# TensorE's projections on other slots, and one state transposed per slot

## What is computed

```python
x = x + _L0_attn_ref(_layernorm(x, axis=-1), ...)
x = x + _L0_ffn_ref(_layernorm(x, axis=-1), ...)
...
xz = x @ in_proj_w.T
xc, z = jnp.split(xz, 2, axis=-1)
...   # u: full convolution over 4 tokens and 512 channels of xc
dt = jnp.clip(jax.nn.sigmoid(u @ dt_w.T + dt_b), 0.0001, 1.0)
A = -jnp.exp(A_log)
Bm = u @ B_w.T
Cm = u @ C_w.T
def step(state, inp):
    dA = jnp.exp(jnp.clip(dtt[:, :, None] * A, -5.0, 5.0))
    dB = dtt[:, :, None] * bt[:, None, :] * ut[:, :, None]
    state = dA * state + dB + 1e-06
    y = jnp.sum(state * ct[:, None, :], axis=-1) + D * ut
...
y = y * jax.nn.silu(z)
return y @ out_w.T
...   # ffn: top 2 of 8 experts by softmax, silu(gate) * up, down; plus a gated shared expert
```

## Time and profile before

| | |
|---|---|
| median of 3 runs | 2993.37 us (2986.91 to 2995.44) |
| profiled execution | 2990.34 us |
| its span, first to last instruction | 2988.5 us |
| mean granted clock of TensorE | 0.915 of full |
| PE busy | 2630.8 us, 88% |
| PEld busy (weight loads) | 2312.5 us, 77% |
| DVE busy | 2249.8 us, 75% |
| ACT busy | 2033.5 us, 68% |
| POOL busy | 2235.5 us, 75% |

### The profile page before, as it was taken

One profiled execution on the slowest core, in us unless ns is written; L12 is line 12 of the kernel. 1 busy time (PEld: TensorE's weight loads), 2 busy tenths in 40 slices (PEclk: granted clock), 3 DMA queues, 4 the chain that ended last, 5 costly groups with the idle time before them and its releaser, 6 DMA issues. The chain is left out here.

```text
span 2988.5 us, 49244 instructions
## 1 busy us (share of the span) xinstructions
PE 2630.8 (88%) x15616; PEld 2312.5 (77%) x15616; DVE 2249.8 (75%) x4890; ACT 2033.5 (68%) x4675; POOL 2235.5 (75%) x1354
## 2 busy tenths in 40 slices
PE   7888898889888888988988888898886599999998
PEld 4777787778777777877877877887875488888887
DVE  2999889988998999899889989998999233333332
ACT  3987888888878888788878878888876133333332
POOL 2999888988888889889889988898887033333333
PEclk9999989998999888899899899888997699999999
DMA  4222222222222222222222222222221278888886
GB/s 168 82 75 76 75 82 76 75 75 90 88 80 79 75 79 89 76 76 85 79 76 75 76 82 75 75 89 87 78 74 41 75 199 201 202 201 202 198 204 152
DMA packets 138185, 309.67 MB, mean 104 GB/s; under 512 B 15041, under 2 KB 79681, under 8 KB 137793
## 3 DMA queue, kind: packets, MB, share of 16 engines
q1 hardware_dynamic: 110848, 270.03, 28.9%
q0 software_dynamic: 27072, 36.46, 6.2%
HBM read 258.42 MB, written 48.01 MB: 103 GB/s over the span
## 5 line engine op out<-in xcount | busy, mean ns | idle before, releaser
L1032 POOL TENSOR_TENSOR room<-dtu,b_all 128x1024 f32<-128x1024 f32 x512 | 1202.3, 2371 | 32.4 <-DVE dtu L1420 14.1
L810 ACT ACTIVATE bank<-room,eps_col 128x512 f32<-128x512 f32 x1024 | 695.2, 685 | 294.6 <-DVE carry L1257 200.3
L794 ACT ACTIVATE room<-room,neg_a 128x256 f32<-128x256 f32 x2048 | 868.8, 499 | 0.8 <-DVE room L1209 0.8
L600 PE MATMUL bank<-ident,room 128*128 128x128 f32 x4096 | 550.9, 291 | 242.7 <-DVE room L1252 220.1
L600 PEld LDWEIGHTS bank<-ident,room 128*128 128x128 f32 x4096 | 495.3, 150 | 295.9 <-DVE room L1252 238.8
L1021 POOL TENSOR_TENSOR room<-room,c_all 128x1024 f32<-128x1024 f32 x224 | 530.9, 2370 | 159.3 <-DVE bank L1243 59.8
L1243 DVE TENSOR_TENSOR_SCAN bank<-room,carry,bank 128x256 f32<-128x256 f32 x864 | 580.3, 735 | 54.5 <-ACT bank L810 53.7
L1157 POOL DMA_INDIRECT out<-room,ids x144 | 223.8, 1554 | 410.1 <-DMA out<-room,ids 192.9
L1322 DVE SCALAR_TENSOR_TENSOR hid<-hid,bank 128x256 f32<-128x256 f32 (+1 forms) x312 | 131.0, 420 | 453.5 <-ACT hid L905 421.2
L1243 DVE TENSOR_TENSOR_SCAN room<-room,carry,bank 128x256 f32<-128x256 f32 x672 | 445.7, 726 | 0.7 <-DVE hot L1293 0.5
L552 PE MATMUL bank<-xnT,w_conv 128*128 128x256 f32 x3072 | 404.2, 288 | 7.0 <-ACT xnT L833 5.5
(11 more groups left out here) (150 smaller groups left out, 3151.0 us busy)
## 6 DMA issues: line engine op xcount, KB each, us to landing
b_all<-b_scratch SPq DMA_DIRECT2D x128, 512.0 KB, 3.9
c_all<-b_scratch SPq DMA_DIRECT2D x128, 512.0 KB, 5.1
room<-in_wgu SPq DMA_DIRECT2D x72, 704.0 KB, 5.8
room<-in_wd SPq DMA_DIRECT2D x72, 384.0 KB
room<-x_by_expert SPq DMA_DIRECT2D x72, 260.0 KB
x_in<-in_x SPq DMA_DIRECT2D x32, 256.0 KB, 5.9
x<-in_x SPq DMA_DIRECT2D x32, 256.0 KB, 2.7
out<-x SPq DMA_DIRECT2D x32, 256.0 KB, 4.2
```

The costliest lines, as they stand in the source:

```text
L600: last = mm(tr_bank[k][:, b * P:(b + 1) * P], v[n % VRING][:, b, k * P:(k + 1) * P], ident[:, :], is_transpose=True, start=False, stop=(n ...
L794: last = af(da[n % RING][:, b, :], dt[c.par][:, b, :], ACT.Exp, scale=neg_a[:, b, n:n + 1])
L810: af(v_slot(c, n, h)[:, :], v[n % VRING][:, 2 * h:2 * h + 2, :].rearrange("p b t -> p (b t)"), ACT.Identity, bias=eps_col[:, 0:1]).then_in ...
L1032: nc.gpsimd.tensor_tensor(out=v[n % VRING][:, :, :], in0=dtu[:, :, :], in1=row, op=ALU.mult) \
```

## The change

- `CONV_SLOT` becomes [0, 4, 5] and holds the last three groups. The first group of a chunk is done at slot 15 of the round before, when the chunk is still in the norm role; for chunks 0 and 1 it is called in `start`.
- b and c go from slot 5 to 7, dt from 6 and 7 to 7 and 8, z from 9 and 10 to 10 and 11, gate and up from 11, 12, 13 to 12, 13, 14, on TensorE.
- ScalarE takes the results at 1 and 6 (uT), 7 (b and c), 8 and 9 (dt), 11 and 12 (z). The gates are at 13, 14, 15 on ScalarE and VectorE. VectorE's `proj_dt` goes to 9 and 10, `proj_gate` to 12, `low_normed` from 15 to 14.
- TensorE transposes state n at slot n + 2, one in each slot. Before, it did two in every even slot. States 14 and 15 stay at slot 0 of the next round.

```diff
-GU_SLOT, GATE_SLOT = [11, 12, 13], [12, 13, 14]
+GU_SLOT, GATE_SLOT = [12, 13, 14], [13, 14, 15]
-CONV_SLOT, Z_SLOT = [0, 1, 3, 4], [9, 10]
+CONV_SLOT, Z_SLOT = [0, 4, 5], [10, 11]
+DT_SLOT, BC_SLOT = [7, 8], 7
...
                 if slot in CONV_SLOT:
-                    n = CONV_SLOT.index(slot)
+                    n = CONV_SLOT.index(slot) + 1
                     proj_conv(c, n // 2, n % 2)
-                if slot == 5:
+                if slot == BC_SLOT:
                     proj_bc(c)
-                if slot in (6, 7):
-                    proj_dt(c, slot - 6)
+                if slot in DT_SLOT:
+                    proj_dt(c, DT_SLOT.index(slot))
...
+                    proj_conv(Chunk(0, 0), 0, 0)
                     for slot in range(NS):
                         project(Chunk(0, 0), slot)
                     proj_norm(Chunk(0, 1))
+                    proj_conv(Chunk(0, 1), 0, 0)
...
-                        if slot > 0 and slot % 2 == 0 and scan:
+                        if slot > 1 and scan:
                             state_transpose(scan, slot - 2)
-                            state_transpose(scan, slot - 1)
...
+                        if norm and slot == 15:
+                            proj_conv(norm, 0, 0)
...
-                if slot in (2, 5):
-                    h = slot // 3
+                if slot in (1, 6):
+                    h = slot // 6
...
-                if slot in (7, 8):
-                    h = slot - 7
+                if slot in (8, 9):
+                    h = slot - 8
...
-                if slot == 6:
+                if slot == 7:
...
-                if slot in (10, 11):
-                    k = slot - 10
+                if slot in (11, 12):
+                    k = slot - 11
...
-                        if slot == 8:
+                        if slot == 9:
                             decays(Chunk(0, 0), 0)
...
-                        if proj and slot in (8, 9):
-                            proj_dt(proj, slot - 8)
-                        if proj and slot == 11:
+                        if proj and slot in (9, 10):
+                            proj_dt(proj, slot - 9)
+                        if proj and slot == 12:
                             proj_gate(proj, 0)
                             proj_gate(proj, 1)
-                        if norm and slot == 15:
+                        if norm and slot == 14:
                             low_normed(norm)
```

## The result

The changed kernel takes **3018.5 us** (median of four runs, 3016.4 to 3021.1), against 2993.2 of the kernel before, run beside it on the same chip (2986.9 to 2995.4). The ratio is 1.0088 with a 95% interval of 1.0071 to 1.0106, so it is slower by 25 us, a little under 1%. That is outside my range and on the other side of my forecast. The profiled execution took 3021.1 us (span 3019.4), 30.8 more than the one before.

What follows compares the result with a forecast made beforehand. No engine owns the loop; VectorE's short repeated waits hang on a chain through the others. Terms 0.98 + 0.8 + 0.5 - 0.6 - 1.4 = 0.3 us mid-sequence, mean 0.5, 15 us over 30 chunks: 2978 us, range 2950 to 3012.

Steps and rivals of the forecast that it cites:

- A: Rival, chance 0.18: bc waits for later uT, TensorE's clock falls, dt and z are late; 1.7 us per chunk, 3029.
- Against it: one wait of 3.29 us left the clock at 1.00: Argument against the clock-fall rival: in the trace before, a 3.29 us wait did not lower TensorE's clock.
- two idle stretches of 3.6 us with little between them: Argument for the clock-fall rival: these TensorE idle stretches bring the clock down at 1044, full again from 1054.
- One transpose per slot: TensorE's state transposes cost the same and GpSimd's buffers keep over 2 us at most slots: zero on both sides.
- The conv group to slot 15: Conv falls into TensorE's wait for state 15, so VectorE's output-product wait goes: gain 0.98 us per chunk.
- Conv and two transposes just fit: On TensorE, 3.2 + 0.95 + 0.95 us fit between second and third gate; down starts at about 0.15.
- uT later: uT's second half behind both ScalarE copies shortens VectorE's state 7 waits from 1.93 to 1.16: gain 0.8 us.
- b/c and dt later: VectorE no longer waits for dt's tanh, 0.6; state 9's second copy stays late: gain 0.5 us.
- z later: VectorE's wait for the second z's tanh after state 12 grows to 0.95 us: loss 0.6 us per chunk.
- The low part a slot earlier: VectorE waits 1.3 us, 1.4 with overlap, for ScalarE's copy behind state 14's products: loss 1.4 us per chunk.
- a low clock over dt's matmuls: Sign named as showing the forecast wrong, on TensorE: it would mean the clock-fall rival; no size given.
- z's wait far over 1 us: Sign named as showing the forecast wrong, on VectorE: ScalarE would be further behind than the prediction's walk.

Runs made afterwards that it cites:

- e1: The changed kernel plus 13 throwaway matmuls per chunk on TensorE ahead of b/c, while it waits for uT: 2973.9 us.
- e11: The kernel before with single transposes and gates' tanh first, plus later slots for conv's last two groups, b/c, dt, z, gate/up; nothing in slot 15: 2938.8 us.
- e7: The kernel before with single transposes, conv group in slot 15, low part at 14, xn taken first, uT's first half at slot 1; other slots old: 2988.8 us.
- e3: The kernel before with one state transposed in every slot, two slots behind, and nothing else of the change: 2948.5 us.
- e6: The changed kernel with two states transposed in every even slot again, all else as changed: 3046.0 us.
- e9: e7 plus 13 throwaway matmuls on TensorE between the last conv group and b/c: 2925.8 us.
- e4: The changed kernel with uT's second half back at ScalarE's slot 5, all else as changed: 2959.8 us.
- e13: The changed kernel with xn taken before slot 14's eps copies, gates' tanh first, and uT's second half at ScalarE's slot 5; no throwaway matmuls: 2879.7 us.
- e10: The changed kernel with throwaway matmuls before b/c, xn taken before slot 14's eps copies, and gates' tanh before the slot's first eps copy: 2900.3 us.
- e2: The changed kernel with ScalarE taking xn (halo and high part) before the eps copies of slot 14: 2948.5 us.
- e14: The changed kernel with xn taken before slot 14's eps copies and gates' tanh first, uT's second half left at slot 6; no throwaway matmuls: 2926.7 us.
- e5: The changed kernel with both the throwaway matmuls ahead of b/c and xn taken before the eps copies of slot 14: 2930.4 us.

## Why the prediction was wrong, step by step

**The rival that happened: A.** Its place, order of events and price were right. I gave it 0.18, and it holds in 27 of 31 chunks. The price was 1.7 us a chunk, 51 in all. Measured: 45 us by e1, which only adds work, over 27 chunks 1.7 us each; in the followed chunk b/c takes 1.11 us more and the first dt group 0.64, 1.75 together. The price was a choice between 0.9 and 2.7, so that it fits so well is partly luck. Without the clock, then, the change gains 18 to 19 us (e1 against before), about my 15, but by other terms than mine, and that is luck too.

The step that failed is the clock's cost over b/c and dt, which the sum left at nothing by "Against it: one wait of 3.29 us left the clock at 1.00". That one wait was an exception, and it isn't the longest that began at full clock, as the heading of the earlier trace rows has it. The wait of 3.60 us for state 14's product began at full clock too. It ended at 1043.95, and the clock was down before TensorE idled again:

```profile
1043.95 1.65 PE L600 MATMUL bank<-ident,room 128*128 128x128 f32 x8 [3.60 <-DVE room L1252]
```

```profile
1044.00:1045.00 1.00, 1.00 (x7) 1.00 (x8) 0.55 (x2) 0.97 (x5) 1.00 (x1) 0.66 0.00 0
1045.00:1046.00 1.00, 0.61 (x3) 0.20 (x1) 1.00 (x3) 1.00 (x3) 0.65 (x2) 0.50 0.00 0
```

So "two idle stretches of 3.6 us with little between them" was a misreading: the first was enough. In the loop of before, 31 waits of 3 us or more for a product of L1252 begin at full clock, and after 24 of them it falls. Ahead of b/c, e11 shows the fall after a single wait of 2.01 us (18 chunks of 21), and e7 after one of 3.3 us (20 of 21), the very length that the forecast rested on. The clock can fall without any wait as well: the second z product of before takes 2.60 us at the low clock, and TensorE was busy without a pause for the 5 us ahead of it, with transposes and routing products of 8 columns.

The Trainium skill, "TensorE: Matmul & The Clock Gate", section "HAM oscillation", takes a single long idle gap as what costs the clock, and I let it stand for the forecast. The trace disagrees: no gap ahead of b/c is longer than 2.01 us, and the clock fell. Its section "A second HAM failure mode: psum-queue depth-cycling" names frequent short idles between groups of matmuls. That is nearer to what the runs show, though in e11 a single one was enough.

**One transpose per slot: "at zero on both sides".** It gains 43 us alone (e3) and 27 within the change (e6). I had looked at what a transpose costs and at who waits for a transposed state (GpSimd), and not at what stands behind a pair in TensorE's queue, dt above all. This is the largest term of the change for good, and I missed it. A good half of what the clock took (45) was thus given back by a term that I had at nothing.

**The conv group to slot 15: gain 0.98.** The wait of the output product went, as forecast. "Conv and two transposes just fit" did not hold: the moved group comes right after 3.90 us of waiting and runs partly at the lower clock, 4.45 us in place of 3.2. Down so starts 1.20 us into the chunk, as before (1.23), not at 0.15. The transposed y was in time all the same, since down itself now takes 2.76 us where it took 4.56: ScalarE copies it at 7.77 us into the chunk, forecast 8.1. What I had not seen at all is the other end: the time freed between conv and b/c is idle time, because b/c waits for uT and not for conv. e7 and e9 price this at up to 63 us.

**uT later: gain 0.8.** State 7 is better than forecast, 0.72 us with an overlap of 0.1, for 1.16. But the same move is what opened b/c's gap, and by e4 its sum is a loss of 59 us: 45 by the clock, and 14 (e4 against e1) to 21 (e13 against e10) because b/c and dt wait for uT even at full clock. I had the gap in the text (idle 1.0, work 1.4, idle 2.2; measured 1.50, 1.5, 2.01) and gave its own length no price at all: "dt late" stood in the rival alone, as the clock's.

**b/c and dt later: gain 0.5.** dt's wait on VectorE went, as forecast (0.6). State 9 waits as before, 0.7, and state 11 waits another 0.70 (the start at 1115.18) that wasn't there. The term is about zero.

**z later: loss 0.6.** The wait rose to 1.93 us, not to 0.95. (In the followed chunk of before it is 0.40 at 1101.87; the 0.28 of the prediction is the chunk ahead of it.) With uT at its old slot (e4) the waits at z are 17.1 us over the stretch, 41.6 in the changed kernel and 16.2 before: what z lost is uT's and the clock's, passed on by dt's tanh, and a loss of z's own slot isn't to be seen. The term was put on the wrong slot.

**The low part a slot earlier: loss 1.4.** Right: 1.28 us in each chunk, 28.5 us over the stretch (22 waits). e2 shows that taking it away is worth more than itself, since it also shortens the wait ahead of the moved conv group (84.1 to 56.2 us) and lifts the clock.

**What would show it.** L1278's wait gone, the low wait of 1.3, bc's wait up to 2.2 and the loop's clock above 0.90 were all named as signs that the forecast is right, and all are there in a kernel that is slower. Of the signs for the forecast only the period of 70.6 failed (71.67). Beside it the two signs named as wrong ("a low clock over dt's matmuls", "z's wait far over 1 us") told the cases apart.

What stays open: why the spell leaves 19 of the 27 chunks in e2, and 10 of them in e14, though b/c's wait there is unchanged in length in nearly all chunks. In every run here the work between conv and b/c's wait is transposes, so whether other work there would have kept the clock up isn't tested, but for the throwaway matmuls. No run separates conv's group from the low part in the changed kernel.

## What to carry to other kernels

On TensorE price an idle time with what comes right behind it: a wait of 2.0 us behind a few transposes made the next two groups take 1.75 us more, and the chain of their consumers (here dt's tanh, z's tanh, VectorE) passed on nearly all of it. So before moving such a group later, or its predecessor away, look where its operand is made, and move this first. A group of equal pieces in one slot is not neutral in an in-order queue: half the transposes ahead of dt was worth 27 to 43 us with the same work. And where two engines alternate, the copy that another engine stands for goes ahead of the one that refills a buffer: that gave 28 us on e3 and 30 on e5, but only 7.5 on e9.

## What the hardware showed that I had not expected

- Throwaway matmuls in that gap made a kernel in which TensorE is the busiest engine (88%) faster by 45 us (e1), and another, e7, by 63 us (e9).
- A higher mean clock (0.93 for 0.90 in the loop) went with a longer time. What counts, as I read it, is where the low spell falls: over groups that others wait for, as b/c and dt are here, or over work that has time.
